# Sixteen experts on every row, or the four chosen ones on gathered rows in tiles of 256

## The reference

```python
combine = _route(x, gate_weight)        # 16 scores a row, the best 4 of the 2 best groups are kept
up = einsum('th,ehi->eti', x, expert_up)             # 16 experts, 256 -> 128
down = einsum('eti,eih->eth', silu(up), expert_down) # 128 -> 256
moe_out = einsum('te,eth->th', combine, down)        # combine is zero for 12 of 16 experts
shared = silu(x @ shared_up) @ shared_down           # 256 -> 512 -> 256
x = x + gb * (moe_out + shared)
```

## Time and profile before

| what | value |
|---|---|
| time, median of 3 runs | 3199.44 us (3190.8 to 3223.53) |
| profiled execution | 3187.41 us, span 3185.6 us |
| `mix_and_experts` | from 1550.6 us to the end, 1635 us |
| of that, the first unit's mix alone | to 1641 us |
| PE busy from 1700 to 3185 us | 1462.09 of 1485 us, granted clock 0.97 |
| DVE, ACT, POOL busy in it | 938.58, 486.66, 304.74 us |
| DMA in it | share 0.10, 34 GB/s |

### The profile page before, as it was taken

How to read it: one execution, slowest core, us unless ns; L and a number is a source line. 1 busy time by engine, 2 the same in 40 slices (tenths; PEclk the granted TensorE clock), 3 DMA queues, 4 the chain that set the end, 5 groups by cost and what they waited for, 6 DMA issues and landing times.

```text
span 3185.6 us, 39962 instructions
## 1 busy us (share of the span) xinstructions
PE 2801.9 (88%) x13712; PEld 2052.0 (64%) x13712; DVE 1650.9 (52%) x4322; ACT 1076.5 (34%) x2142; POOL 618.1 (19%) x417
## 2 busy tenths in 40 slices
PE   4989994444998799999569999999999999999998
PEld 4966663333888678788446666666666666666665
DVE  3448883218142233333246665675656756667655
ACT  1258774233543111111123333323333233333231
POOL 1115552021100100000122122221222212222201
PEclk7579997665555666665679999999999999999999
DMA  3425557765663433434410011110111101111000
GB/s 97 139 93 164 162 172 194 184 131 129 148 140 103 136 108 109 129 87 129 159 40 19 29 47 47 48 47 1 47 47 48 47 1 47 47 47 47 7 1 14
DMA packets 348447, 269.81 MB, mean 85 GB/s; under 512 B 166284, under 2 KB 305996, under 8 KB 346724
## 3 DMA queue, kind: packets, MB, share of 16 engines
q1 hardware_dynamic: 337680, 256.90, 27.9%
q0 software_dynamic: 2304, 8.39, 1.0%
q10 hardware_dynamic: 8276, 2.10, 0.3%
HBM read 166.45 MB, written 100.89 MB: 84 GB/s over the span
## 4 chain that ended last, share of the span: by engine, by line
PE 35%; DVE 7%; POOL 6%; issue 2%; SPq 0%; DMA 0%; ACT 0%; POOLq 0%; DVEq 0%; ACTq 0%
PE mx_dn L1769 12%; PE mx_up L1755 11%; PE mx_m L1708 4%; POOL mx_st L1655 3%; DVE mx_acc L2060 3%; PE mx_m L1709 2%; PE mx_m L1717 2%; PE mx_m L1732 2%; POOL mx_rms L1666 1%; DVE mx_t L1922 1%; PE mx_m L1746 1%; POOL mx_acc L1673 1%; PE mx_m L1718 1%; POOL mx_acc L1676 1%; DVE mx_t L1943 1%
## 5 line engine op out<-in xcount | busy, mean ns | idle before, releaser
L2060 DVE SCALAR_TENSOR_TENSOR mx_acc<-mx_dn,mx_comb,mx_acc 128x256 f32<-128x256 f32 x1024 | 424.4, 477 | 476.5 <-PE mx_dn L1769 474.4
L1769 PE MATMUL mx_dn<-mx_edn,mx_hs 128*128 128x256 f32 x2048 | 513.3, 395 | 3.2 <-ACT mx_hs L1838 3.2
L1769 PEld LDWEIGHTS mx_dn<-mx_edn,mx_hs 128*128 128x128 f32 x2048 | 398.0, 197 | 168.2 <-issue 95.0
L1755 PE MATMUL mx_up<-mx_h2T,mx_eup 128*128 128x512 f32 x1024 | 496.2, 608 | 0.0
L1838 ACT ACTIVATE mx_hs<-mx_up 128x512 f32<-128x512 f32 x320 | 190.0, 596 | 789.8 <-PE mx_up L1755 789.5
L1755 PEld LDWEIGHTS mx_up<-mx_h2T,mx_eup 128*128 128x128 f32 x1024 | 189.2, 192 | 156.2 <-issue 147.0
L652 DVE SCALAR_TENSOR_TENSOR cv_acc<-cv_pre,conv_w,cv_acc 128x512 f32<-128x512 f32 x288 | 215.7, 750 | 88.8 <-ACT cv_acc L574 82.0
L516 PE MATMUL cv_pj<-cv_hT,wqkv 128*128 128x512 f32 x384 | 182.2, 605 | 13.4 <-ACT cv_acc L574 7.3
L1442 ACT ACTIVATE ds_U<-ds_ups 64x256 f32<-64x256 f32 x64 | 24.1, 377 | 419.0 <-PE ds_ups L1335 419.0
L1660 POOL TENSOR_TENSOR mx_t<-mx_vf,mx_ids 128x1024 f32<-128x1024 f32 x16 | 31.5, 1966 | 645.9 <-DVE mx_pr L1917 645.9
L1195 DVE TENSOR_TENSOR ci_prod<-ci_Ad,ci_T 128x62 f32<-128x62 f32 (+15 forms) x124 | 67.0, 540 | 148.9 <-DMA ci_Ad<-diag_d 144.6
(11 more groups left out here) (227 smaller groups left out, 4783.9 us busy)
## 6 DMA issues: line engine op xcount, KB each, us to landing
kqT_d<-cv_kqc SPq DMA_DIRECT2D x16, 1024.0 KB, 8.0
vf_d<-cv_vf SPq DMA_DIRECT2D x16, 1024.0 KB, 5.3
ds_kqT<-kqT_d SPq DMA_DIRECT2D x16, 1024.0 KB, 5.8
mx_vf<-vf_d SPq DMA_DIRECT2D x16, 1024.0 KB, 6.2
fl_toep<-taps_d SPq DMA_DIRECT2D x32, 392.0 KB, 5.1
fl_pool<-vf_d SPq DMA_DIRECT2D x8, 1216.0 KB
xin<-_attn_hidden_states_dram SPq DMA_DIRECT2D x16, 512.0 KB, 3.8
hT_d<-hT SPq DMA_DIRECT2D x16, 512.0 KB, 2.6
```

The lines of the kernel that those rows point to most:

```text
L1755: ins = pe.matmul(up_ps[x % 2][:], lhs, h2T[i][:, k, :], start=(k == 0), stop=(k == KD - 1))
L1769: ins = pe.matmul(dn_ps[(i + n) % 2][:, j, :], hs[x % 4][:, j * P:(j + 1) * P], rhs, start=(x == 0 and j % 2 == 0) or x >= NS, stop=(x >= ...
L2060: ins = dve.scalar_tensor_tensor(out=acc[i][:, j, :], in0=dn_ps[(i + n) % 2][:, j, :], scalar=comb[i][:, j, e:e + 1], in1=acc[i][:, j, :], ...
```

## The change

The stage is written anew around choosing rows.

- **Places.** For each unit DVE counts (`rank`), with the help of five small matmuls (`count`), where each row's four copies go in a list by expert. POOL writes the normalised rows there, in device memory (`X_d`), with 16 indirect DMAs of 128 rows a unit (`scatter`). After the fourth unit of a sequence (a **batch**, b) `tables` works out which expert each of 48 tiles of 256 rows belongs to and where it begins, and SP fills the gaps behind each expert's rows with zeros (`pads`, 16 DMAs).
- **Tiles.** For each of the 48 tiles of a batch, SP reads a table entry into a register and loads 256 rows, reads another and loads that expert's up weights. PE turns the tile (`turn`, 4 transposes), ACT modulates it, PE multiplies up (`raise_`, two matmuls of 256 columns), ACT takes the Silu, PE reads the expert from the table and multiplies down (`lower`, two of 256), ACT or DVE takes the result out of PSUM, and SP stores it (`Y_d`). In beat n, PE has turn n, up n - 2 and down n - 4. A batch always has its 48 tiles, 192 in all.
- **Sums.** POOL gathers four rows for each row of the batch (`gather`, 16 indirect DMAs a unit), and DVE adds them with their weights to the shared expert's result (`total`), which like the sum after attention is now kept in device memory.
- **Order.** There are 24 bodies of 16 beats now, all written out. Body u (batch b, g = u mod 4) has the shared expert of unit u in its first four beats if b < 4, one tile of batch b - 1 in each of the other twelve if b is 1 to 4, and the sums of unit u - 8 if b is 2 to 5. The mix is spread over three bodies: body u holds steps 19 to 39 of unit u + 1, steps 0 to 18 of unit u + 2, and the routing and scattering of unit u. The two products of step 18 that POOL had are DVE's. Inputs of a unit have one buffer, not two.

```diff
@@ -28,6 +28,11 @@
...
+TT = 2 * P
+NTL = 48
+CAP = L + TT
+SPARE = 16 * TT
+ROWS = E * CAP + SPARE
...
+    NX = NS + PER
+    LAG = 2
...
+            def pads(b):
+                sp.wait_ge(tab_done, b + 1)
+                if b >= 2:
+                    sp.wait_ge(xT_done, NTL * (b - 1))
+                for e in range(E):
+                    r = sp.value_load(tab_p[b % 2][0:1, e:e + 1], min_val=0, max_val=2 * ROWS - TT)
+                    sp.dma_start(m.X_d[bass.ds(r, TT), :].rearrange("(j p) d -> p j d", p=P),
+                                 zrow[:].unsqueeze(1).to_broadcast([P, 2, D])).then_inc(pad_out, 16)
...
+            def xload(n):
+                b, t = n // NTL, n % NTL
+                r = sp.value_load(tab_s[b % 2][0:1, t:t + 1], min_val=0, max_val=2 * ROWS - TT)
+                if n >= RX:
+                    sp.wait_ge(xT_done, n - RX + 1)
+                sp.dma_start(xt[n % RX][:], m.X_d[bass.ds(r, TT), :].rearrange("(j p) d -> p j d", p=P))\
+                    .then_inc(xt_in[n % RX], 16)
+                e = sp.value_load(tab_e[b % 2][0:1, t:t + 1], min_val=0, max_val=E - 1)
+                if n >= RE:
+                    sp.wait_ge(tup_done, n - RE + 1)
+                sp.dma_start(eup[n % RE][:], w.expert_up[bass.ds(e, 1)].squeeze(0).rearrange("(k p) i -> p k i", p=P))\
+                    .then_inc(eup_in[n % RE], 16)
...
+            def ystore(n):
+                b, t = n // NTL, n % NTL
...
+                sp.wait_ge(yt_done[n % 2], n // 2 + 1)
+                sp.dma_start(m.Y_d[b % 2][t * TT:(t + 1) * TT, :].rearrange("(j p) d -> p j d", p=P), yt[n % RY][:])\
+                    .then_inc(yt_out[b % 2][n % RY], 16)
...
+            def scatter(u, j):
+                b = u // UB
...
+                for k in range(TOPK):
+                    n = column(u, j, k)
+                    pool.indirect_dma_start(m.X_d[:, :], bass.IndirectOffsetOnAxis(ap=idx[b % 2][:, n:n + 1], axis=0),
+                                            xn[u % 2][:, j * D:(j + 1) * D], None).then_inc(scat[u % 2], 16)
...
+            def gather(v, j):
+                b, n = v // UB, v * J + j
...
+                if n >= 2:
+                    pool.wait_ge(sum_done, n - 1)
+                for k in range(TOPK):
+                    c = column(v, j, k)
+                    pool.indirect_dma_start(G[n % 2][:, k, :], None, m.Y_d[b % 2][:, :],
+                                            bass.IndirectOffsetOnAxis(ap=idy[b % 3][:, c:c + 1], axis=0))\
+                        .then_inc(G_in[n % 2], 16)
...
+            for b, g, u in bodies():
+                v = u - 2 * UB
+                early = b >= 2 and g > 0
+                late = b >= 2 and g == 0
+                if u + 1 < NU:
+                    rms_root(u + 1)
+                if early:
+                    gather(v, 0)
+                if u + 2 < NU:
+                    deviations(u + 2)
+                if early:
+                    gather(v, 1)
+                if u + 1 < NU:
+                    ln_root(u + 1)
+                if early:
+                    gather(v, 2)
+                    gather(v, 3)
+                if late:
+                    for j in range(J):
+                        gather(v, j)
+                if b < B:
+                    for j in range(J):
+                        scatter(u, j)
...
+            def turn(n):
+                pe.wait_ge(xt_in[n % RX], 16 * (n // RX + 1))
...
+                for k in range(KD):
+                    for j in two:
+                        ins = pe.transpose(xT_ps[n % 2][:, k * TT + j * P:k * TT + (j + 1) * P],
+                                           xt[n % RX][:, j, k * P:(k + 1) * P], m.ident[:])
+                ins.then_inc(xT_done, 1)
...
+            def raise_(n):
+                pe.wait_ge(hTt_done, n + 1)
+                pe.wait_ge(eup_in[n % RE], 16 * (n // RE + 1))
...
+                for k in range(KD):
+                    ins = pe.matmul(up_ps[n % 2][:, 0:TT], eup[n % RE][:, k, :], hTt[n % RH_][:, k, :],
+                                    start=(k == 0), stop=(k == KD - 1))
+                ins.then_inc(tup_done, 1)
...
+            def lower(n):
...
+                e = pe.value_load(tab_e[b % 2][0:1, t:t + 1], min_val=0, max_val=E - 1)
+                pe.wait_ge(tsilu_done, n + 1)
+                if n >= 2:
+                    pe.wait_ge(yt_done[n % 2], n // 2)
+                for j in two:
+                    ins = pe.matmul(dn_ps[n % 2][:, j * D:(j + 1) * D], hst[n % RS][:, j * P:(j + 1) * P],
+                                    edn[:, bass.ds(e, 1), :].squeeze(1), start=True, stop=True)
+                ins.then_inc(tdn_done, 1)
...
+                    n = u * PER - NTL + x - NS
+                    if b < B and x < NS:
+                        if x < NS - 1:
+                            up(u, x + 1, raised)
+                        down(u, x, turned)
+                    if 1 <= b <= B and x >= NS:
+                        turn(n)
+                        if n >= LAG:
+                            raise_(n - LAG)
+                        if n >= 2 * LAG:
+                            lower(n - 2 * LAG)
+                    if u + 1 < NU:
+                        if x == 4:
+                            mix(u + 1, 29)
+                        if x == 5:
+                            mix(u + 1, 30)
+                    if u + 2 < NU:
+                        if x == 6:
+                            mix(u + 2, 7)
+                        if x == 7:
+                            mix(u + 2, 8)
+                            mix(u + 2, 9)
+                        if x == 8:
+                            mix(u + 2, 10)
+                            mix(u + 2, 11)
+                        if x == 9:
+                            mix(u + 2, 14)
+                            mix(u + 2, 15)
+                    if b < B and x == 10:
+                        count(u)
+                    if u + 1 < NU:
+                        if x == 11:
+                            mix(u + 1, 35)
+                        if x == 12:
+                            mix(u + 1, 38)
...
+            def keep_odd(n):
...
+
+            def total(v, j):
+                b, n = v // UB, v * J + j
+                q = n % 2
+                s = n * 5
+                dve.wait_ge(G_in[q], 16 * TOPK * (n // 2 + 1))
+                dve.wait_ge(c_in[q], 32 * (n // 2 + 1))
+                for k in range(TOPK):
+                    if k:
+                        dve.wait_ge(sum_step, s + k)
+                    c = column(v, j, k)
+                    dve.scalar_tensor_tensor(out=co[q][:], in0=G[q][:, k, :], scalar=wts[:, b % 3, c:c + 1],
+                                             in1=co[q][:], op0=ALU.mult, op1=ALU.add).then_inc(sum_step, 1)
+                dve.wait_ge(sum_step, s + 4)
...
+                    n = u * PER - NTL + x - NS
+                    if u + 1 < NU:
+                        if x == 0:
+                            mix(u + 1, 19)
+                            mix(u + 1, 21)
+                        if x == 1:
+                            mix(u + 1, 23)
+                        if x == 2:
+                            mix(u + 1, 25)
+                    if b < B and x < NS:
+                        route(u, x)
+                    if u + 2 < NU:
+                        if x == 3:
+                            mix(u + 2, 0)
+                        if x == 4:
+                            mix(u + 2, 1)
+                    if 1 <= b <= B and x >= NS and n >= 2 * LAG and n % 2 == 1:
+                        keep_odd(n - 2 * LAG)
+                    if u + 1 < NU:
+                        if x == 5:
+                            mix(u + 1, 29)
+                        if x == 6:
+                            mix(u + 1, 31)
+                        if x == 7:
+                            mix(u + 1, 33)
+                    if u + 2 < NU:
+                        if x == 9:
+                            mix(u + 2, 15)
+                        if x == 10:
+                            mix(u + 2, 17)
+                            mix(u + 2, 18)
+                    if b < B and x == 11:
+                        rank(u)
+                        if g == UB - 1:
+                            tables(b)
+                    if b >= 2 and x in sums(g):
+                        total(v, sums(g).index(x))
```

738 lines of the change are left out of this document (528 added, 210 removed).

## The result

The changed kernel takes **3543.32 us** (median of 4 runs, 3537.38 to 3555.99) beside 3204.68 for the kernel before (4 runs): ratio 1.1058, 95% interval 1.0989 to 1.1127. The forecast was 3240 us and the range ended at 3480. The direction was right, the size was not. The profiled execution has a span of 3554.2 us, 369 more than before's 3185.6.

A forecast was written before the change was run, and what follows sets the result against it. PE bounded the kernel before; afterwards a POOL/DVE loop of 75.7 us a body, 83.3 with tiles, would. Loops, batch starts, last batch, end and 25 us of register reads gave a 3225 us span, forecast 3240 us, range 3030 to 3480.

The forecast's parts named there:

- The loop, steps 1 to 8: Chain through each body, POOL's root to POOL's 16 scatter issues: 75.7 us without tiles, 83.3 us with them.
- S: POOL's issue of one indirect DMA: taken as 1.1 us, between bounds of 0.75 and 1.97.
- step 4: PE's link of the loop, the mix's steps 7 to 15: 23.4 us, or 27 with three tiles among them.
- the rest is covered by it: In each body, gathers, DVE's sums (11 us) and SP's issues (some 27 us) lie beside the loop; PE idles about 15 us.
- Batch starts: Extra time beyond the loops: 5 us at batch 1's start, 8 more in batch 2.
- The last batch: After bodies 14 and 15's mix: 105 us to the first tile, then 48 tiles at 3.3 us each and 10 to empty.
- The end: After the last tile: 64 gathers at 1.1 us and 8 us of landing, sum and store.
- Register reads: Table entries read on PE and SP: 0.3 us each in the beats that matter, 25 us; 50 by the page.
- Cheap issue: Rival: POOL's indirect DMA costs 0.75 us like the plain one, giving 3140 us; chance 0.27.
- PE the bound: Rival: PE stays the bound, bodies cost 69 us with tiles and 58 without, giving 2980 us; chance 0.09.
- Clock: Rival: PE's idle time leaves it at 1.2 GHz, step 4 grows by 20 us in ten loops, 3500 us; chance 0.10.
- DVE holding up POOL: Rival: DVE's two-input operations hold up POOL's reading of places, S goes to 2.0, 3500 us; chance 0.12.

The follow-up runs named there:

- the front early: Changed kernel with the next unit's steps 19 to 23 moved from the next body's head to beats 12 to 14 of this one; 3343 us, ratio 1.043.
- the root in the scatter: Changed kernel with those steps early, plus POOL's next rms root issued in the middle of the 16 scatters; 3275 us, ratio 1.0199.
- four buffers: Root-in-scatter kernel with four, not two, buffers for gathered rows, kept results and inputs of the sums, some fetched earlier; 3223 us, on another chip 3351.
- the loads on ACT: Changed kernel with the four loads of the next mix's inputs issued by ACT at beat 13 instead of SP; 3378 us, ratio 1.0547.
- the doubled scatter: Changed kernel with every scatter issued a second time into an unused tensor, 16 more indirect DMAs a body; 3639 us, ratio 1.1368.
- the constant rows: Root-in-scatter kernel with SP's rows and up weights from constants, not table reads; 3229 us. Alone on the changed kernel, 3491 us.

## Why the prediction was wrong

- **What bounds before**, PE: nothing contradicts it. **The tile's price on PE**, 2.3 us: right. In body 15, beside no mix, beats follow each other in 2.17 us where rows are there (PE's rows of the changed kernel):

```profile
3182.00 0.60 PE L2018 MATMUL mx_sh<-ident,mx_xt 128*128 128x128 f32 x4
3182.44 1.03 PE L2028 MATMUL mx_up<-mx_hTt,mx_eup 128*128 128x256 f32 x4
3183.30 1.03 PE L2043 MATMUL mx_dn<-mx_edn,mx_hst 128*128 x4
3184.17 0.60 PE L2018 MATMUL mx_sh<-ident,mx_xt 128*128 128x128 f32 x4
```

- **The loop, steps 1 to 8**: right link by link where it closes, 78.1 for 75.7 and, with the front early, 88 for 83.3. Sizes: S 1.26 for 1.1, and PE's step 4 30.7 for 27, since PE's matmuls there alternate between both levels of the clock (a tile's up part takes 0.87 us at a granted clock of 1.00 and 1.71 at 0.50). I had counted on 0.9 and more; batches 1 to 3 had 0.80.
- **The step that failed is "the rest is covered by it".** I followed one loop and took every other chain in the body for shorter. In bodies with tiles the additions, the square and the sum of the next unit (steps 19 to 23) stand at the head of the next body, on DVE behind its last tile and on ACT behind the shared expert's first parts, and these stand on PE behind all twelve tiles. So a second loop goes through the *whole* body. Most of its length could have been worked out by my own terms: 24 us to PE's step 7, 27 to step 15, 4 for counts, transposes and gate, six more tiles 14, 10 from the shared expert's first matmul to the root, 79 us; with the waits for DVE's read of the counts (5.1) and ACT's turn at the body's end (I put it at 5) that its chain showed, 89, more than my 83.3. In the changed kernel it took 105.8 us. PE's 70 us a body I used only as a busy time. Moving these steps, with the root in the scatter and four buffers, gave 187 us within one job.
- **A larger part of the 22 us a body is the place.** Three numbers split them. The first loop by itself took 88 us and not 83.3: 5 us of sizes. With the loads on ACT and no long sequencer instructions the second loop was 92.4 us, and the root waited 4.2 us for DVE and not 18.8: 4 us more. The last 13 us come only in the changed kernel's places:

```profile
L1842 POOL TENSOR_TENSOR mx_rms<-mx_rms,half_pow x2: 2973/2973/2973, 2175.5 to 2267.9; 128x16 f32<-128x16 f32 x2
...
  DVE mx_rms L2325: 8.3, 2
```

- **These 13 us are hardly the loads' queue.** The kernel with the doubled scatter has its loads on SP and its front late, like the changed kernel, and no long sequencer instruction. A root started at 2287.34 us. The next root stood behind the scatter until 2395.61, but DVE had its input ready long before (POOL's and DVE's rows of that kernel):

```profile
2287.34 2.93 POOL L1844 TENSOR_TENSOR mx_rms<-mx_rms,half_pow 128x16 f32<-128x16 f32 x1
...
2377.60 0.31 DVE L2316 TENSOR_SCALAR mx_rms<-mx_rms 128x16 f32<-128x16 f32 x1
```

From one root to the input of the next are 90.6 us here, and 89.0 to 90.6 in the four bodies of batch 1, against 104.5 to 106.1 in the changed kernel. So the second loop is some 90 us with the loads on SP, close to the first loop's 88, and the 165 us that the moved loads seemed to gain were mostly the place. One reservation stays: POOL paces that kernel's bodies at 107 us, which leaves its transfers more time than bodies of 92 us would. The place costs the bodies little where the second loop does not bind: the kernel with four buffers had bodies of 85.1 us in batch 1 in such a place and 83.4 elsewhere.
- **An estimate from these rows**: the changed kernel in a place without long sequencer instructions. From body 4's root to body 14's it would take what the kernel with the loads on ACT took (938 us for 1073), and behind the last root it would take what the doubled scatter's kernel took less 16 issues (454.5 - 20.2 = 434 for 468). That is 3543 - 135 - 34, some 3375 us, still 135 above the forecast. No run measured it.
- **Batch starts**: 7 and 10 us for 5 and 8 (the first was 1 us in the two other profiles of this kernel). **The last batch**: 163 and 201 us for 108 and 168. Up to the first tile PE stands still for 19.5 us at body 14's end, and the 16 zero fills took 26.4 us. In the eleven kernels without long sequencer instructions they took 19.1 to 20.2 us, about 1.25 each, so my 1.3 was right and the rest is the place. With the loads on ACT, where no sequencer instruction was long, it was still 128 us for the 108 and 188 for the 168: that part is my sum's. The tiles ran at 231 GB/s, SP's reads among them (27 us behind the last root by the constant rows, 44 us in the changed kernel: 424 for 468). **The end**: 104 us for 78. The 64 issues are 81 us at 1.26 and not 70, and the two buffers cost 9 (94.0 for 102.9 with four).
- **Register reads**: on PE nothing, as the beats above show. On SP 25 us was the right size, nearly all of it in the last batch's 48 tiles and none in the bodies. The Trainium skill, "DMA: Bandwidth & Descriptors", section "Latency and other measured facts", has a floor of about 600 ns; here a read takes 0.27 us in the median on SP, so the trace does not agree, and the term by the page, 50 us, would have been too much.
- **Rivals.** Cheap issue: no, S is dearer. PE the bound: no. Clock: it fell to 0.80, but the price was 3.7 us a body and not 20. DVE holding up POOL: at the head of five bodies two gathers beside DVE's 128x1024 operations took 1.91 to 1.97 us each and the next ones 0.95, so it exists, but the mean of all 512 issues is 1.0. By the rule of the Trainium skill, "SBUF — State Buffer", section "Who interferes with whom", the trace agrees for these ten.
- **What would show it**: "if POOL's roots come before DVE needs them, so is it [wrong]" was close. It was the reverse, the root waiting for DVE, that showed the second loop at a glance. DMA share was 0.55 in the third batch where I had 0.8.
